# A graph layer with experts: another order in the prologue, gate columns first, and residuals of the last tiles on TensorE

## The chip, the cores and the metric
One core of a Trainium2 chip. The metric is the device time of one execution in microseconds, the lower the better; three executions of the kernel before took 656.91, 658.34 and 659.75 us (median 658.34).

## The reference
2500 nodes with 512 numbers each, 80000 edges (src, dst), sorted by dst. All in fp32.

```python
h = layernorm(x)
agg = segment_sum(h[src], dst, 2500)
x = x + relu((h + agg) @ W1 + b1) @ W2 + b2          # W1, W2: 512 x 512
t = layernorm(x)
gate = softmax(t @ Wg)                               # 8 experts
topv, topi = top_k(gate, 2); topv /= sum(topv) + 1e-6
x = x + sum_e score_e * (gelu(t @ W1[e] + b1[e]) @ W2[e] + b2[e])   # 512 -> 256 -> 512
```

## The kernel before, in words
Every engine has one program, written by hand in a fixed order; engines wait for each other on semaphores. An engine runs its instructions strictly in that order. The nodes are cut into 20 tiles of 125 rows (P = 125, T = 20). For x itself, row p * 20 + t belongs to tile t.

Stage 1, the first layer (0 to about 132 us). z = layernorm(x) @ W1 is computed before the neighbours are summed, since the sum is linear. VectorE takes the row statistics of a batch of tiles (`statistics`, BATCHES), ScalarE the root (`roots`), VectorE the reciprocal and shift (`scales`). ScalarE writes the normal rows xn (`normal_rows`, three buffers); TensorE turns them (`turn_normal`, four transposes); ScalarE copies the f16 upper part (`normal_columns`, xT_top) and VectorE takes the rest (`low_columns`, xT_rest). `first_layer(t)` on TensorE is 3 x 8 matmuls of up to 264 columns (top x W1_hi, top x W1_lo, rest x W1_hi), with `turn_normal(t + 1)` after the first 8. 8 of the columns are the gate's. `split_z` on ScalarE evicts z; GpSimd subtracts for z_lo. W1 itself is first scaled by powers of two per column: sums of absolute values (`W1_abs`, on TensorE), then `invert_scale`, `scale_weights`, `first_high` and `first_low`; `centre_gate` does the same for the gate weights.

The neighbour sum is a product with a matrix of counts. The edges are cut into 125 windows of 20 destination nodes. dst and src are loaded; for each edge a key and a source row are formed (`edge_sources`, `edge_keys`) and stored to HBM (edge_pairs). `find_chunk` finds for each window the chunk of 128 edges in which it begins, GpSimd gathers these chunks' dst rows (bound_rows), `find_starts` counts the exact start, and GpSimd gathers each window's edges as slot_rows from edge_pairs. `compare_edges`, `smallest` and `close_rows` test that the edges are of the expected form, and give a flag that goes through HBM (range_d) to all engines (a general path is taken where it is set; it isn't here). The slot rows are turned (`turn_rows`, after tile ROWS_AT = 5) and unpacked (`take_rows`). From tile FLAG_AT + 1 = 8 on, TensorE does some windows after each tile: VectorE makes the one-hots of a window (`one_hots`, hot_key and hot_lo; a ring of four), TensorE multiplies them (`window`, 6 matmuls), ScalarE evicts the counts (`take_counts`). 25 windows lie beside the tiles 8 to 19, two in each and three in the last.

Stage 2 (about 136 to 412 us). Five groups of 500 nodes: `sums_tile` multiplies z_hi and z_lo by the counts, beside it the windows of the next group; `relu`, `relu_high`, and `mlp2(g, q)`, 24 matmuls for each of the four tiles q of a group, columns 256 to 519 (gate columns among them) before 0 to 255. `logits_of` takes logits, the top 8 and their indices; `residual` adds x_res (x + b2, summed by GpSimd) to the product in PSUM, with bn_stats and bn_aggr; `std2` and `residual_end` give 1/std; `norm2` writes the normal rows xt. SP stores x and xt and loads the next residual rows.

Stage 3, the passage (412 to 458 us). For the last group `mlp2` writes to banks of its own, 0 to 7. With all 20 tiles' choices VectorE forms `chosen` and `either`; TensorE ranks them (two matmuls), VectorE computes places, at_tile, token_part and at_row; TensorE spreads them (40 matmuls), and the token lists go to GpSimd's gathers. route_tables are constants that GpSimd writes after its last residual sum. SP loads the experts 0 to 3 (512 KB twice each), then stores, expert 4, the last stores, waits until all of x has landed (x2_landed), then experts 5 to 7. ScalarE splits the weights (`split_high_up`, `split_high_down`), VectorE their lower parts.

Stage 4 (458 to 655 us): 27 blocks of 256 rows, with gathers and adds to HBM by indirect DMA. It isn't changed.

## Time and profile before

| | us |
|---|---|
| median of three executions | 658.34 |
| the profiled execution, its own time | 657.24 |
| its span, first to last instruction | 655.5 |
| TensorE busy | 555.8 (85%) |
| VectorE busy | 413.9 (63%) |
| ScalarE busy | 316.7 (48%) |
| GpSimd busy | 251.2 (38%) |
| the chain that ended last: TensorE | 50% |
| DMA, VectorE, GpSimd, ScalarE in it | 13%, 12%, 10%, 7% |

The page also has the span in 40 equal slices of 16.4 us. Each digit is the busy share in tenths, PEclk the granted TensorE clock in tenths of full speed:

```profile
PE   4776877799999999999999999925999999999900
DVE  5866574687369777976986131589566664554541
ACT  2573766533252125124322300558776766777671
PEclk9997899999899999999999999965999999999955
DMA  8160600020020310211122113779688989899995
```

The first eight slices are the first layer, slices 9 to 25 the neighbour sums with TensorE full, slices 26 to 28 the passage, then the experts. A busy share says how much an engine did, not what it waited for; the rows further down name that.

### The profile page before, as it was taken

The numbers are of one execution on the slowest core, as the hardware profiler recorded it, in microseconds if no ns is written. First come the engines' busy times: TensorE is split into PE (matmuls) and PEld (weight loads), VectorE is DVE, ScalarE is ACT, GpSimd is POOL, SyncE is SP. The second block draws the span as 40 slices with busy tenths as digits, with TensorE's granted clock in tenths as the row PEclk, the third lists the DMA queues.
The fourth block names the chain that finished last, engine by engine and source line by source line (L and its number), as shares of the span: only waits on it lengthen the run. The fifth ranks groups of instructions, "written<-read, shape, count | busy, mean of one in ns | idle before, by whom it ended". The sixth has DMA issues, their size and how long they took to land.

```text
span 655.5 us, 10719 instructions
## 1 busy us (share of the span) xinstructions
PE 555.8 (85%) x3842; PEld 435.9 (67%) x3843; DVE 413.9 (63%) x805; ACT 316.7 (48%) x579; POOL 251.2 (38%) x219
## 2 busy tenths in 40 slices
PE   4776877799999999999999999925999999999900
PEld 2666767656756766766666665725989998889800
DVE  5866574687369777976986131589566664554541
ACT  2573766533252125124322300558776766777671
POOL 4450222203016005100700331025567877778763
PEclk9997899999899999999999999965999999999955
DMA  8160600020020310211122113779688989899995
GB/s 259 54 161 1 192 1 1 1 75 1 1 64 2 95 48 12 84 48 49 49 77 65 39 58 96 262 236 304 139 172 183 186 167 193 187 205 198 165 185 76
DMA packets 40302, 71.91 MB, mean 110 GB/s; under 512 B 10313, under 2 KB 14545, under 8 KB 39714
## 3 DMA queue, kind: packets, MB, share of 16 engines
q0 software_dynamic: 12704, 29.22, 22.6%
q1 hardware_dynamic: 26257, 37.34, 19.3%
q10 hardware_dynamic: 1288, 4.66, 2.4%
q8 instruction: 32, 0.52, 0.3%
q14 instruction: 21, 0.17, 0.1%
HBM read 46.07 MB, written 26.69 MB: 111 GB/s over the span
## 4 chain that ended last, share of the span: by engine, by line
PE 50%; DMA 13%; DVE 12%; POOL 10%; ACT 7%; issue 6%; SPq 1%; ACTq 0%; POOLq 0%; DVEq 0%
PE psum L1414 26%; PE psum L1398 9%; PE psum L1451 7%; POOL out_x L601 6%; DMA out_x<-y,target_i 6%; PE psum L1330 3%; POOL xg L594 3%; DVE hot_key L1047 2%; DMA slot_rows<-edge_pairs,start_i 2%; DVE hot_lo L1047 2%; DMA xg<-xt_d,token_i 2%; DMA b_now<-in_L_ffn_b 2%; DVE xT_rest L891 1%; DVE stat L861 1%; ACT y L823 1%
## 5 line engine op out<-in xcount | busy, mean ns | idle before, releaser
L663 ACT ACTIVATE counts<-psum 128x400 bf16<-128x400 f32 x125 | 62.6, 504 | 163.2 <-PE psum L1398 162.9
L1047 DVE TENSOR_TENSOR hot_key<-iota_key,key_w 128x1200 f16<-128x1200 f16 x125 | 105.7, 845 | 47.3 <-PE psum L1398 47.3
L1414 PE MATMUL psum<-counts,z_hi 125*128 125x500 bf16 x400 | 101.8, 375 | 1.6 <-ACT h L687 1.6
L601 POOL DMA_INDIRECT out_x<-y,target_i x54 | 88.5, 1639 | 36.3 <-SPq L480 15.0
L1414 PE MATMUL psum<-counts,z_lo 125*128 125x500 bf16 x400 | 101.5, 377 | 0.0
L1398 PE MATMUL psum<-hot_key,hot_lo 128*128 128x200 f16 x750 | 84.3, 250 | 15.6 <-DVE hot_lo L1047 14.9
L1398 PEld LDWEIGHTS psum<-hot_key,hot_lo 128*128 128x128 f16 x750 | 65.2, 98 | 39.0 <-issue 18.8
L566 POOL TENSOR_TENSOR h_lo<-h,h_hi 128x500 fp32r<-128x500 f32 x16 | 23.5, 1499 | 169.5 <-ACT h_hi L694 169.5
L1047 DVE TENSOR_TENSOR hot_lo<-iota_lo,lo_w 128x768 f16<-128x768 f16 x125 | 83.5, 668 | 0.0
L1414 PEld LDWEIGHTS psum<-counts,z_lo 125*128 125x128 f16 x400 | 39.3, 98 | 45.7 <-issue 1.1
L594 POOL DMA_INDIRECT xg<-xt_d,token_i x54 | 57.4, 1063 | 31.2 <-issue 15.5
L1261 DVE TENSOR_TENSOR he_lo<-he,he_hi 128x256 fp32r<-128x256 f32 x54 | 23.0, 425 | 66.1 <-ACT he L816 66.1
L1414 PEld LDWEIGHTS psum<-counts,z_hi 125*128 125x128 f16 x400 | 37.8, 98 | 29.3 <-ACT h L687 1.8
L1547 PE MATMUL psum<-xT_hi,w_hi 128*128 128x256 f32 x192 | 54.4, 283 | 0.3 <-DVE xT_lo L1243 0.3
L553 POOL TENSOR_TENSOR z_lo<-z,z_hi 125x512 f16<-125x512 f32 x20 | 26.9, 1352 | 71.8 <-ACT z L656 71.8
L1547 PE MATMUL psum<-xT_hi,w_lo 128*128 128x256 f32 x192 | 54.4, 283 | 0.0
L1547 PE MATMUL psum<-xT_lo,w_hi 128*128 128x256 f32 x192 | 54.4, 283 | 0.0
L823 ACT ACTIVATE y<-y,slot_score 128x512 f32<-128x512 f32 x54 | 36.0, 714 | 33.2 <-DVE y L1270 33.2
L569 POOL TENSOR_TENSOR x_res<-x_res,b_row 125x512 f32<-125x512 f32 x20 | 29.3, 1484 | 48.8 <-DMA x_res<-in_x 48.8
L1558 PE MATMUL psum<-w_hi,he_hi 128*128 128x512 f32 x96 | 40.1, 417 | 3.5 <-DVE he_lo L1261 3.1
L1270 DVE TENSOR_TENSOR y<-psum,b_now 128x512 f32<-128x512 f32 x54 | 34.6, 683 | 9.9 <-DMA b_now<-in_L_ffn_b 6.4
L1451 PE MATMUL psum<-W_hi,h_hi 128*125 128x264 f32 (+1 forms) x128 | 37.9, 296 | 0.0
(252 smaller groups left out, 1149.9 us busy)
## 6 DMA issues: line engine op xcount, KB each, us to landing
w_raw<-in_L_ffn_W SPq DMA_DIRECT2D x16, 512.0 KB, 6.8
b_now<-in_L_ffn_b SPq DMA_DIRECT2D x27, 256.0 KB, 4.9
x_res<-in_x SPq DMA_DIRECT2D x20, 224.0 KB
out_x<-x SPq DMA_DIRECT2D x20, 224.0 KB
xt_d<-xt SPq DMA_DIRECT2D x20, 224.0 KB
x_in<-in_x SPq DMA_DIRECT2D x2, 1120.0 KB
W_raw<-in_L_gnn_W ACTq DMA_DIRECT2D x2, 1024.0 KB, 5.4
out_x<-in_x SPq DMA_DIRECT2D x1, 1536.0 KB, 11.7
```

Of the source, the lines that this page charges most:

```text
L569: pool.tensor_tensor(x_res[:, q], x_res[:, q], b2_row[:], ALU.add).then_inc(S["res_sum"], 1)
L594: pool.indirect_dma_start(out=xg[:, k % XB, i], out_offset=None, in_=xt_d[:, :], in_offset=bass.IndirectOffsetOnAxis(ap=token_i[:, 2 * k + ...
L601: pool.indirect_dma_start(out=out[:, :], in_=y[:, k % YB, i], in_offset=None, out_offset=bass.IndirectOffsetOnAxis(ap=target_i[:, 2 * k + ...
L663: act.activation(counts[:, it % 2, :, place:place + W], psum[:, WIN + w % 2, 0:MW].rearrange("p (w h) -> p h w", w=W), ACT.Copy).then_inc( ...
L823: act.activation(y[:, k % YB, i], y[:, k % YB, i], ACT.Copy, scale=slot_score[:, 2 * k + i:2 * k + i + 1])\
L1047: ins = dve.tensor_tensor(hot[:, w % RING].rearrange("p s (n two) -> p s n two", two=2), iota[:].rearrange("p (o n two) -> p o n two", o=1 ...
L1270: dve.tensor_tensor(y[:, k % YB, i], psum[:, 4 + i], b2_now[:, k % 2], ALU.add).then_inc(taken, 1)
L1398: ins = mm(psum[:, WIN + w % 2, a * MH:(a + 1) * MH], hot_lo[:, w % RING, k], hot_key[:, w % RING, k], start=(k == 0), stop=(k == SL - 1))
L1414: ins = mm(psum[:, AGG + c, 0:GN], half[:, t, c * 128:(c + 1) * 128], counts[0:P, g % 2, t], start=(t == 0 and n == 0), stop=(t == T - 1 a ...
L1451: ins = mm(psum[0:P, bank + b, 0:columns.stop - columns.start], h_[:, k, rows], w_[:, k, columns], start=(k == 0 and n == 0), stop=(k == K ...
L1547: ins = mm(psum[:, 2 + m, 0:B], w_[e][:, c, cols], x_[:, c], start=(c == 0 and i == 0), stop=(c == KC - 1 and i == 2))
L1558: ins = mm(psum[:, 4 + i, :], h_[:, m, i * 128:(i + 1) * 128], w_[e][:, m], start=(m == 0 and n == 0), stop=(m == HC - 1 and n == 2))
```

## The change
It has two parts.

Prologue: the batches of row statistics are (0,2), (2,4), (4,6) and on as before. ScalarE, not VectorE, forms the edges' source rows, in three passes, before roots(0). VectorE's order puts statistics and W1's scaling first, and find_chunk(0) and (1) after low_columns(1). xn is written densely, and the turn reads it with a stride. TensorE does W1's sums before the edges' spans, and 6 + 3 extra matmuls whose result nobody reads (`stay_warm`). ROWS_AT and FLAG_AT are one tile later, so that windows begin with tile 9. In the tiles with windows VectorE makes the one-hots before low_columns(t + 1). Batch 5 of x is loaded from ScalarE's queue instead of SP's.

Passage: for the last four tiles the gate columns of all come before the other columns, and all their logits are taken together (`last_logits`). For tiles 17 to 19 TensorE adds the residual with an fp32 product by the identity, ScalarE takes the row statistics (`last_rows`), and VectorE only the reciprocal (`last_scale`). The load of the last residual rows comes before the store of tile 15. The first half of token_part is computed on VectorE; ScalarE splits experts 1 to 3 after the last normal rows.

```diff
-BATCHES = ((0, 1), (1, 3), (3, 6), (6, 10), (10, 15), (15, 20))
+BATCHES = ((0, 2), (2, 4), (4, 6), (6, 10), (10, 15), (15, 20))
-ROWS_AT, FLAG_AT, ROWS_FIRST = 5, 7, 4
+ROWS_AT, FLAG_AT, ROWS_FIRST = 6, 8, 4
...
+            sp.wait_ge(S["x2_ready"], 4 * (G - 1))
+            load_residual(G - 1, 3)
             store(G - 2, 3)
-            load_residual(G - 1, 3)
             store(G - 1, 0)
...
-                act.activation(xn[:, t % 3].rearrange("p (c q) -> p c q", c=KC), x_in[:, t % (2 * HALF)].rearrange("p (q c) -> p c q", c=KC),
-                               ACT.Identity, scale=rstd1[:, t:t + 1], bias=shift1[:, t:t + 1]).then_inc(S["xn_ready"], 1)
+                act.activation(xn[:, t % 3], x_in[:, t % (2 * HALF)], ACT.Identity, scale=rstd1[:, t:t + 1], bias=shift1[:, t:t + 1])\
+                   .then_inc(S["xn_ready"], 1)
...
+            act.wait_ge(S["src_in"], 32)
+            step(act.activation(pairs_sb[:, :, 1], src_i[:], ACT.Identity, scale=1.0 / T, bias=half_down[:]))
+            step(act.activation(pairs_sb[:, :, 1], pairs_sb[:, :, 1], ACT.Identity, bias=turn_up[:]))
+            act.activation(pairs_sb[:, :, 1], pairs_sb[:, :, 1], ACT.Identity, bias=turn_down[:]).then_inc(S["sources_ready"], 1)
+            roots(0)
             first_high(0)
-            roots(0)
...
+                for b in range(1, len(BATCHES)):
+                    if t + 2 == BATCHES[b][0]:
                         roots(b)
...
+            def last_rows(q):
+                n = 4 * (G - 1) + q
+                act.wait_ge(S["mlp2_done"], n + 1)
+                act.wait_ge(x2_out[q], 64 * (G - 1))
+                step(act.activation(x2[:, q].rearrange("p (b n) -> p b n", b=2), last_out(q), ACT.Copy, accum_out=last_ln[:, q, 0:1]))
+                step(act.activation(last_ln[:, q, 1:2], last_ln[:, q, 0:1], ACT.Copy, scale=-1.0 / D))
+                step(act.activation(xt[:, q], x2[:, q], ACT.Square, bias=last_ln[:, q, 1:2], accum_out=last_ln[:, q, 2:3]))
+                act.activation(last_ln[:, q, 3:4], last_ln[:, q, 2:3], ACT.Sqrt, scale=1.0 / D, bias=eps_t[0:P, 0:1]).then_inc(S["std2_ready"], 1)
...
             std2(G - 2, 3)
             split_high_up(0)
             norm2(G - 2, 3)
             split_high_down(0)
+            std2(G - 1, 0)
+            last_rows(1)
             norm2(G - 1, 0)
+            last_rows(2)
+            last_norm(1)
+            last_rows(3)
+            last_norm(2)
+            last_norm(3)
+            for e in range(1, 4):
+                split_high(e)
...
-            centre_gate()
-            find_chunk(0)
+            largest()
+            statistics(0)
             invert_scale()
             scale_weights(0)
-            statistics(0)
             scale_weights(1)
             scales(0)
             scale_weights(2)
             scale_weights(3)
+            centre_gate()
             first_low(0)
             first_low(1)
-            find_chunk(1)
             low_columns(0)
+            edge_keys()
             statistics(1)
             scales(1)
-            edge_sources()
             low_columns(1)
-            edge_keys()
+            find_chunk(0)
+            find_chunk(1)
+            low_columns(2)
             statistics(2)
-            low_columns(2)
             scales(2)
+            low_columns(3)
             scale_back()
             find_starts()
...
             for t in range(FLAG_AT + 1, T):
+                for w in range(counted(t - 1), counted(t)):
+                    one_hots(w)
                 if t + 1 < T:
                     low_columns(t + 1)
-                for w in range(counted(t - 1), counted(t)):
-                    one_hots(w)
...
+            def stay_warm(n):
+                for k in range(n):
+                    mm(psum[:, SM + 1], part16[:].broadcast_to([128, 128]), W1_abs[:, k % KC], start=True, stop=True)
...
+            stay_warm(6)
             turn_normal(0)
+            stay_warm(3)
...
+            def add_residual(q):
+                pe.wait_ge(S["res_sum"], 4 * (G - 1) + q + 1)
+                for b in range(2):
+                    ins = mm(psum[0:P, 2 * q + b, 0:DH], ident[0:P, 0:P], x_res[:, q, b * DH:(b + 1) * DH],
+                             start=False, stop=True, skip_group_check=True)
+                ins.then_inc(S["mlp2_done"], 1)
...
+            for q in (2, 3):
+                if q == 3:
+                    pe.wait_ge(S["x2_ready"], 4 * (G - 1))
+                for k in range(KC):
+                    ins = last_gates(q, k)
+            ins.then_inc(S["gate_columns"], 1)
+            for k in range(KC):
+                last_halves(1, k)
+            pe.wait_ge(S["x2_ready"], 4 * (G - 1) + 1)
             pe.wait_ge(S["chosen_ready"], 1)
             pe.wait_ge(S["route_tables"], 1)
             choices = either[:].rearrange("p n e -> p (n e)")
             mm(psum[0:P, 0, 0:T * NE], before[:], choices, start=True, stop=True)
             mm(psum[0:P, 1, 0:T * NE], ones16[:], choices, start=True, stop=True).then_inc(S["ranked"], 1)
+            add_residual(1)
+            for q in (2, 3):
+                for k in range(KC):
+                    last_halves(q, k)
+                add_residual(q)
```

## Rows read from the trace of the kernel before
**Rows 1.** Busy time by stretch: start:end, length, each engine busy, PEclk, DMA share, GB/s.
```profile
70.00:128.00 58.00, 44.41 (x403) 40.19 (x400) 33.90 (x62) 39.86 (x73) 14.62 (x10) 1.00 0.12 37
424.00:458.00 34.00, 14.97 (x134) 14.25 (x133) 30.41 (x88) 24.57 (x31) 11.70 (x19) 0.61 0.88 278
```
**Rows 2.** The chain of waits, one first-layer tile: start us, us, what.
```profile
99.74 0.68 PE psum L1398 x6
100.42 0.89 PE psum L1330 x8
101.30 0.44 PE psum L1308 x4
101.77 0.60 ACT xT_top L646
102.39 0.68 DVE xT_rest L891
...
104.22 0.69 DVE hot_key L1047
104.91 0.48 DVE hot_lo L1047
...
105.53 0.68 PE psum L1398 x6
```
**Rows 3.** The chain of waits in the prologue.
```profile
26.21 0.68 DVE xT_rest L891
...
34.71 14.76 DMA slot_rows<-edge_pairs,start_i
```
**Rows 4.** The timeline of 10 to 25 us: start us, us, engine, line, operation.
```profile
16.07 1.30 ACT L639 ACTIVATE xn<-x_in,shift,rstd 125x512 f32<-125x512 f32 x1
...
19.20 1.99 PE L1330 MATMUL psum<-W_hi,xT_top 128*125 128x256 f16 x8 [0.68 <-ACT xT_top L646]
19.25 1.08 DVE L918 CAST chunk_i<-first 125x2 int32<-125x2 f32 x1
...
23.25 1.44 POOL L535 DMA_INDIRECT bound_rows<-in_dst,chunk_i  x1 [0.30 <-issue]
```
**Rows 5.** From the tiles bound_rows and slot_rows: time from issue to landing.
```profile
DMA to landing us min/median/max: 3.5/3.5/3.6
...
DMA to landing us min/median/max: 8.0/11.4/14.8
```
**Rows 6.** Timelines of TensorE, VectorE and GpSimd at the first layer's end.
```profile
131.87 1.20 PE L1398 MATMUL psum<-hot_key,hot_lo 128*128 128x200 f16 x12
...
135.78 1.01 PE L1414 MATMUL psum<-counts,z_hi 125*128 125x500 bf16 x4
...
128.47 1.73 DVE L1047 TENSOR_TENSOR hot_key<-iota_key,key_w 128x1200 f16<-128x1200 f16 x1
...
128.03 1.53 POOL L553 TENSOR_TENSOR z_lo<-z,z_hi 125x512 f16<-125x512 f32 x1 [4.25 <-ACT z L656]
```
**Rows 7.** The chain of waits in the passage.
```profile
426.65 2.87 DMA x_res<-in_x
...
434.35 0.33 DVE tile_count L1152
...
437.47 0.78 DVE picked L1168 x2
...
442.30 3.01 DVE at_row L1195 x5
...
458.75 3.14 PE psum L1547 x24
```
**Rows 8.** The timeline of ScalarE in the passage.
```profile
423.27 0.82 ACT L673 ACTIVATE xt<-x,ln,rstd 125x512 f32<-125x512 f32 x1
...
426.85 1.04 ACT L698 ACTIVATE w_hi<-w_raw 128x1024 fp32r<-128x1024 f32 x1
...
445.05 1.28 ACT L781 ACT_TABLE_LOAD   x1
```

More of the change, by code:

```diff
@@ L717, in _ @@
             normal_columns(0)
-            roots(1)
             normal_rows(1)
@@ L722, in _ @@
                     normal_columns(t + 1)
-                for b in range(2, len(BATCHES)):
-                    if t == max(BATCHES[b][0] - 3, 1):
+                for b in range(1, len(BATCHES)):
+                    if t + 2 == BATCHES[b][0]:
                         roots(b)
@@ L1119, in _, with last_logits, last_scale @@
                             residual_end(g - back, q)
+            def last_logits():
+                dve.wait_ge(S["gate_columns"], 2)
+                for q in range(4):
+                    n = 4 * (G - 1) + q
+                    ins = dve.tensor_tensor(logits[:, n], psum[0:P, 2 * q + 1, DH:DH + NE], gate_in[:, n], ALU.add)
+                step(ins)
+                for n in range(4 * (G - 1), T):
+                    ins = dve.max(top[:, n], logits[:, n])
+                step(ins)
+                for n in range(4 * (G - 1), T):
+                    ins = dve.max_index(topi[:, n], top[:, n], logits[:, n])
+                step(ins)
+            def last_scale(q):
+                n = 4 * (G - 1) + q
+                dve.wait_ge(S["std2_ready"], n + 1)
+                step(dve.reciprocal(rstd2[:, n:n + 1], last_ln[:, q, 3:4]))
+                dve.tensor_tensor(last_ln[:, q, 4:5], last_ln[:, q, 1:2], rstd2[:, n:n + 1], ALU.mult).then_inc(S["shift2_ready"], 1)
             for m in range(KC):
@@ L1123, in _ @@
                 dve.tensor_tensor(last_lo[:, m], h1[:, m], last_hi[:, m].bitcast(F32), ALU.subtract).then_inc(S["h1_split"], 1)
-            logits_of(G - 2, 3)
+                if m == 2:
+                    logits_of(G - 2, 3)
             residual(G - 2, 3)
-            for q in range(3):
-                logits_of(G - 1, q)
-                residual(G - 1, q)
-                residual_end(*((G - 1, q - 1) if q else (G - 2, 3)))
-            residual_end(G - 1, 2)
-            logits_of(G - 1, 3)
+            residual(G - 1, 0)
+            residual_end(G - 2, 3)
+            residual_end(G - 1, 0)
+            last_logits()
             def split_low_up(e):
@@ L1430, in mlp2 @@
             def mlp2(g, q):
-                last = g == G - 1
-                bank = (WIN, AGG, AGG + 2, SM)[q] if last else SM
-                if q == 0 and not last:
+                if q == 0:
                     pe.wait_ge(S["w_split"], 1)
@@ L1497, in _ @@
             mlp2(G - 2, 3)
-            for q in range(4):
-                mlp2(G - 1, q)
+            for k in range(KC):
+                pe.wait_ge(S["h1_split"], 4 * (G - 1) + k + 1)
+                last_gates(0, k)
+                ins = last_halves(0, k)
+                if k == 1:
+                    last_gates(1, 0)
+                if k == KC - 1:
+                    ins.then_inc(S["mlp2_done"], 1)
+                if k >= 1:
+                    last_gates(1, k)
+            for q in (2, 3):
[3 more added lines that the diff above has]
+                    ins = last_gates(q, k)
+            ins.then_inc(S["gate_columns"], 1)
+            for k in range(KC):
+                last_halves(1, k)
+            pe.wait_ge(S["x2_ready"], 4 * (G - 1) + 1)
             pe.wait_ge(S["chosen_ready"], 1)
```

148 lines of the change are left out of this document (73 added, 75 removed).

## The prediction
> **What bounds the kernel now.** First the table by stages: from 70 to 128 us TensorE is busy 44.4 of 58 us at a granted clock of 1.00 (2.4 GHz), so the stretch of tiles 8 to 19 of the first layer is full of waits, while from 424 to 458 us it is busy 15 of 34 us at a mean granted clock of 0.61, since it waits long, and VectorE 30.4 of 34 [rows 1]. The expert loop behind it isn't touched. Between 135.8 us, where the neighbour sums start [rows 6], and 412 us TensorE is fed back to back and the change moves nothing. So two stretches decide: the prologue (0 to 135.8) and the passage to the experts (412 to 458.75).
>
> Then the chain of waits. In one tile of the first layer it goes round: windows 0.68, first third of the layer 0.89, the turn of the next tile 0.44, ScalarE's xT_top 0.60, VectorE's xT_rest 0.68, only then the one-hots, 1.16 each (104.22 to 105.4), and again the windows, at 105.53: 5.79 us from 99.74 to 105.53 [rows 2]. The one-hots of tile t stand behind low_columns(t+1) in VectorE's order, which needs the turn of tile t+1. That is a loop of waits, no engine's work. Ahead of it stands the chain that makes the edge rows: chunk_i done at 20.33, start_i at 32.4, the second gather issued at 34.71 and landed 14.76 us later, at 49.47 [rows 3, 4].
>
> **Prologue, part by part.**
> Early order. Statistics of two tiles, W1's sums and the scaling go ahead of the search for chunks. low_columns(1) ended at 26.89 [rows 3]. I bring it forward by 3.6 to about 23.3: W1's sum no longer waits behind the edge spans (about 1.8 us, an estimate from the order of the steps), and the 24 matmuls of tile 0, at 0.25 each (1.99 for 8, against 0.89 for 8 later: that is the lower of the clock's two levels, 1.2 against 2.4 GHz) [rows 2, 4], take 2.7 instead of 5.5 us if stay_warm does what it says. Bound: 0 to 4 us. Against that stand ScalarE's three passes over the sources, 640 elements each; they were 0.5 us each on VectorE and need at least 0.82 x 640/512 = 1.0 us [rows 8], at most the strided xn's 1.30 x 640/512 = 1.6 [rows 4]. I take 1.2; they start when src has landed (estimate 10 us) and hold roots(0), so that I keep 1 us of the 4.6 for them, which is the 3.6.
> The two find_chunk steps, some 3.1 us, now follow low_columns(1): chunk_i is known at 26.4 instead of 20.33, 6.1 later. Before, the second bound gather was issued at 23.25 and took 3.5 [rows 4, 5]; now 29.35 and 32.9. VectorE used to arrive only at 31.4, so 4.7 of the 6.1 were slack; behind the landing stand a rest of low_columns(3) and the two counts. start_i is at about 34.4, 2 us later than 32.4; the slot gather's second half is issued at 36.7 instead of 34.71 [rows 3].
> Queues. It was slow (14.76) beside dst_next and x_in's batch 4 on SP's queue. The keys leave 8 us earlier, so dst_next is over, and batch 4 is asked for at about 33.6, ahead of the gather. The other half of the gather landed in 8.0 [rows 5]. Bounds 8 and 14.8; I take 10.8, as one of the two disturbers is left: landed at L = 47.5 (44.7 to 51.5) against 49.47.
> From L to the first window. One tile more goes ahead (FLAG_AT 8). By L all of tiles 0 to 6 are done (3.1 us of matmuls each [rows 2], no waits for dst_next now). (These counts are mine, from the order of the program.) After L: close, turn and take the rows, statistics(4), scales(4); these steps took 15 us before and take 12.6 now, as low_columns(8) and one fewer handshake lie between; xn(10) 0.8, turn 0.5, two thirds of the layer 1.8: windows of tile 9 at L + 15.7 = 63.2.
> The loop. VectorE now makes the one-hots of tile t first, while TensorE does tile t. TensorE's own work is 3 x 0.89 + 0.44 + 2 x 0.52 = 4.15 us with two windows [rows 2]; a tile with three windows waits some 0.85 for the counts to be taken, 5.5. ScalarE has 0.48 + 0.75 (xn dense, 0.82 like norm2 [rows 8], instead of 1.30 [rows 4]) + 1.24 + 0.9 = 3.4; VectorE 2 x 1.16 + 0.6 = 2.9. So TensorE sets it: 7 x 4.15 + 2 x 5.5 + 3.7 (no turn) = 43.7, and 2.7 for statistics(5) and its scales, which still stand on VectorE's path: 46.4 to the end of tile 19, at 109.6. Before it was 131.87 [rows 6]. Reading xn with a stride in the turn costs 0.01 to 0.02 per transpose, nothing. The sums start 3.9 later in both. **Gain 22.3 us**, bounds 14 (below) to 26.
>
> Here a rule is weighed. Rows: a hot_key that ran beside a z_lo of GpSimd took 1.73 where it takes 0.69 to 0.77 [rows 2, 6], about 0.95 more. The Trainium skill's GPSIMD Engine Reference (specification table, SBUF interfaces) says that GpSimd shares its SBUF interfaces with VectorE, with contention for instructions with two SBUF inputs, which the one-hots are; by that rule z_lo, which used to fall into VectorE's idle time, now meets a one-hot in each tile. The trace agrees for that row.
> With one meeting in each tile VectorE has 3.9, still under 4.15: hidden, so the sum has nothing for it. Cover gone, it is the first rival.
>
> **Passage to the experts, part by part** (times as if the prologue were unchanged).
> Gate columns first: TensorE has all logits of tiles 16 to 19 by 422.8. VectorE reaches last_logits only at 424.65, since residual_end(G-1,0) waits for a std2 queued on ScalarE behind a split of expert 0, norm2 and another split. 1.8 for logits, max and index, 1.8 for the choice: chosen_ready 428.2 against 431.9.
> But ranking also waits for route_tables, on GpSimd behind x_res of the last tile. That load is now issued at 420.3 instead of 426.26, behind four experts' weights on SP's queue (4.2 MB, an estimate from the sizes has them over at about 426). I take it as landed at 426.7; it was 429.52 [rows 7]. tile_count followed 4.83 behind it, at 434.35 [rows 7]; now 431.5, a gain of 2.85 (0 if the queue is slower, 5.4 if chosen_ready alone decided).
> Residual by TensorE: the first add stands behind the ranking, so mlp2_done(18) comes at 431.5 + its price. No row shows an fp32 matmul that wide. Bounds: two cold passes of 0.25 (0.5) and eight (2.0) [rows 4]; I take 1.5, for fp32 is the slowest type here: 433.0. Then 12 matmuls, cold: 2.9; add 1.2; 12 warmer: 1.5; add 1.0: 437.2 and 439.6.
> ScalarE's last_rows: copy 0.8 with the sum, 0.25, square 0.9, root 0.3, three handshakes: 2.5 (2.1 to 3.0), from 0.82 for 512 elements [rows 8]. std2 of tiles 17, 18, 19 come at 435.6, 439.7, 442.9.
> VectorE waits for each: last_scale(1) comes 2.9 after tile_count (picked was 3.12 after it [rows 7]) at 434.4 and waits 1.2; last_scale(2) 1.8 behind the next step at 437.8 and waits 1.9; last_scale(3), at 441.9, waits 1.1. Then token_part's first half, now on VectorE: 1.0 (0.7 to 1.3); second half 1.3; at_row from 445.8 instead of 442.30, five in 3.0 [rows 7]. So routing is 3.5 us later. Taking away the residuals (three of 1.65) from VectorE is worth nothing here: the waits are longer.
> ScalarE stands idle from 424.3 to 433, with the splits of experts 1 to 3 (six of 1.04, 0.95 apart [rows 8]) queued behind last_norm(3) at 444.4; before, four of the six were in gaps up to 437.6. It gets to Exp at about 451.4 (447.35 before), then the Gelu table 1.28 [rows 8], the splits 4 to 7, 7.6, and xT_hi at 460.9. SP's stores land later, so x2_landed and the last three experts' loads shift too, 448.8 instead of 440.8, which just holds. The first expert matmul, 458.75 [rows 7], is at 462.8. **Loss 4.0 us** (gain 1 to loss 8).
>
> One rule of the ScalarE page is weighed. The rows have a table load of 1.28 where Exp and where Gelu first come [rows 8], none between Sqrt and Copy, Identity or Relu; Square is not in the trace. If it isn't beside Sqrt, each last_rows has two loads: 6 x 1.28 = 7.7 on a chain that VectorE waits for. The Trainium skill (ScalarE: Activation LUTs, Table sets: the hidden batching unit) has the cheap functions in every set, by which there is none. No run here shows it.
>
> **Sum.** The profiled execution took 657.24 us (span 655.5), 0.17% below the median of 658.34. 657.24 - 22.3 + 4.0 = 638.9; on the median's scale 640.
>
> **Rivals.**
> 1. VectorE becomes the bound of the tile loop: two meetings with z_lo in each tile, 2.9 + 1.9 = 4.8 and 6 with three windows, 0.65 more in each of 10 tiles plus the statistics unhidden: +8, 647 to 648. For: z_lo (1.53) is as long as a one-hot pair [rows 6] and starts right when the one-hots do. Against: one z_lo can delay only the instruction it meets. Chance 0.20.
> 2. The passage costs nothing: the fp32 adds are near their lower bound, the clock rises early, and x_res lands when it can. Then 4 to 5 less: 635. For: 8 us of slack on ScalarE. Against: ScalarE's splits stay behind. Chance 0.17.
> 3. stay_warm doesn't raise the clock, or the long gather stays long (L = 51): tile 0 costs 2.8 more, L 3.5 more: 646. Chance 0.13. Square's table loads: 648. Chance 0.04.
> 4. Slower: the new order in the loop turns round on itself. If VectorE falls a whole tile behind, low_columns(t+1) stands behind the one-hots and TensorE's last third waits for it: 0.89 + 0.44 + 0.60 + 2.3 + 1.9 + 0.68 + 0.89 + 1.0 = 8.7 us per tile against 5.79 now [rows 2]. 63.2 + 10 x 8.7 = 150 against 131.87, and 4.0 lost in the passage: 680. It turns to slower from (131.87 - 63.2 - 4.0)/10 = 6.5 us per tile. For it: VectorE's 3.9 is only 0.25 below TensorE's 4.15. Against: it has to lose over 4 us in a row first, and the single burst that there is is statistics(5), 3.4. Chance 0.05.
>
> **How the numbers follow.** Forecast 0.41, around 640 (636 to 644). With the rivals 1, 2 and 3 the range is 632 to 651; above it lie the worst of rival 1 and rival 4, below it both gains at their bounds. 0.5% (3.3 us), about what a measurement of this kernel can tell from no change, is reached by all but rival 4 and a sum of rivals 1, 3 and a passage at -8: faster 0.91, same 0.03, slower 0.06.
>
> **What would show it.** Right: a tile period of 4.1 to 4.7 between 63 and 110 us with TensorE near 95% busy; sums starting at 113 to 114; the slot gather landing near 47; ScalarE idle for 8 us after its first split; first expert matmul 50 us after the sums end instead of 46.4. Wrong: hot_key's mean well over 1 us in the loop (rival 1), a table load in the passage, tile 0's matmuls at 0.25 each, or a gap of TensorE ahead of each last third (rival 4). The prediction fails most easily in the loop: ten tiles carry each error tenfold.

## The result and the profile after

| | before | after |
|---|---|---|
| median, us (20 runs each, 655.14 to 661.31 and 650.93 to 657.60) | 657.84 | 653.96 |
| ratio to before, 95% interval | | 0.9939 [0.9921, 0.9958] |
| the profiled execution, its own time | 657.24 | 656.98 |
| its span | 655.5 | 655.2 |

The change gives 4 us where 18 were forecast, and 653.96 lies above the range (632 to 651). The profiled execution of after lies 3.0 us above its median; all stage times below come from it, so some 3 us of what it lacks against the forecast belong to this one execution.

The 40 equal slices of after, 16.4 us each:

```profile
PE   5788989999999999999999999424999999999900
...
PEclk9899989998999999999999999776899999999965
DMA  8253300200012202211120335379487999899996
```

The first eight slices of TensorE read 57889899 where they read 47768777 before, so the first layer is denser; the dip of the passage is deeper, 424 against 925. Busy time by stretch in after, to be read as [rows 1]: TensorE was busy 77% of 70 to 128 us before, now 90%; in the passage it is 52% of 62 us.

```profile
70.00:120.00 50.00, 45.09 (x412) 43.19 (x411) 44.10 (x71) 34.52 (x76) 16.31 (x12) 0.97 0.03 7
398.00:460.00 62.00, 32.20 (x237) 29.85 (x236) 33.74 (x104) 35.83 (x57) 13.71 (x23) 0.75 0.69 224
```

The same in times. Offsets in the last four rows are counted from the start of the last matmul of the sums (412.23 before, 398.45 after).

| | before | after | the step on record |
|---|---|---|---|
| chunk_i | 20.33 | 27.43 | 26.4 |
| start_i | 32.4 | 37.87 | 34.4 |
| first windows beside a tile | 69.44 (tile 8) | 68.39 (tile 9) | 63.2 |
| sums start | 135.78 | 121.30 | 113.5 |
| tile_count, behind the sums | 22.1 | 21.5 | 19.3 |
| last store of normal rows issued | 25.8 | 35.1 | |
| x2_landed (load of expert 5 issued) | 28.6 | 39.2 | 36.6 |
| first expert matmul | 46.5 | 59.2 | 50.6 |

So in this pair of executions the prologue gives 14.5 us (forecast 22.3) and the passage takes 12.7 of them back (forecast 4.0). The sums (276.5 and 277.2) and the expert blocks (196.8 and 197.6) hardly differ. The chain of waits of after, through the passage (start us, us, what):

```profile
406.92 8.24 DMA x_res<-in_x
415.23 1.26 POOL x_res L578
419.94 1.80 PE psum L1503 x4
433.52 3.91 DMA xt_d<-xt
440.27 13.48 DMA w_raw<-in_L_ffn_W
454.74 1.04 ACT w_hi L710
456.30 1.30 DVE xT_lo L1276 x2
457.64 5.50 PE psum L1620 x24
```

Before, the chain went over at_tile, token_part, at_row and the table load [rows 7, 8], that is over the routing. Now it goes over the residual rows, the adds on TensorE (L1503), the last store, and then the weights of an expert. The weights weren't in the chain before. The prediction had said of their later loading that it "just holds"; it doesn't. ScalarE, which splits each expert's weights in its fixed order, shows it: in after it waits 2.02, 4.26 and 1.89 us for weights on their way (8.2 in all), in the trace of before it doesn't wait for any.

### The profile page after: what moved, and what is told of

Same layout as the page of the kernel before. It is cut to its first block, busy times and chain, and to the rows that moved or that the text cites. A ratio compares the mean times of both kernels' runs of the same rounds, so it can differ in the third digit from the quotient of the medians.

```text
span 655.2 us, 10782 instructions
## 1 busy us (share of the span) xinstructions
PE 565.3 (86%) x3864; PEld 446.1 (68%) x3865; DVE 416.7 (64%) x794; ACT 310.8 (47%) x596; POOL 251.0 (38%) x222
## 4 chain that ended last, share of the span: by engine, by line
PE 51%; DMA 14%; POOL 11%; DVE 7%; issue 7%; ACT 6%; SPq 1%; ACTq 1%; POOLq 0%; DVEq 0%
PE psum L1455 26%; PE psum L1439 9%; POOL out_x L610 7%; PE psum L1483 7%; PE psum L1369 6%; DMA out_x<-y,target_i 5%; POOL xg L603 4%; DMA w_raw<-in_L_ffn_W 2%; DMA xg<-xt_d,token_i 2%; DMA src_i<-in_src 1%; DMA x_res<-in_x 1%; DMA b_now<-in_L_ffn_b 1%; DVE stat L880 1%; PE psum L1347 1%; ACT y L846 1%
## 5 line engine op out<-in xcount | busy, mean ns | idle before, releaser
L1067 DVE TENSOR_TENSOR hot_key<-iota_key,key_w 128x1200 f16<-128x1200 f16 x125 | 107.7, 861 | 49.8 <-PE psum L1439 48.8
L1067 DVE TENSOR_TENSOR hot_lo<-iota_lo,lo_w 128x768 f16<-128x768 f16 x125 | 86.4, 691 | 0.0
L562 POOL TENSOR_TENSOR z_lo<-z,z_hi 125x512 f16<-125x512 f32 x20 | 26.7, 1344 | 52.5 <-ACT z L665 52.5
L1620 PEld LDWEIGHTS psum<-xT_hi,w_hi 128*128 128x128 f32 x192 | 37.8, 197 | 8.9 <-DVE xT_lo L1276 8.0
L1276 DVE TENSOR_TENSOR xT_lo<-psum,xT_hi 128x512 fp32r<-128x512 f32 x56 | 36.1, 686 | 10.4 <-ACT xT_hi L814 8.7
```

Source lines behind the costliest of these rows:

```text
L1067: ins = dve.tensor_tensor(hot[:, w % RING].rearrange("p s (n two) -> p s n two", two=2), iota[:].rearrange("p (o n two) -> p o n two", o=1 ...
L1276: dve.tensor_tensor(xT_lo[:, :, part], psum[:, i].rearrange("p (c n) -> p c n", c=KC), xT_hi[:, :, part].bitcast(F32), ALU.subtract).then_ ...
L1620: ins = mm(psum[:, 2 + m, 0:B], w_[e][:, c, cols], x_[:, c], start=(c == 0 and i == 0), stop=(c == KC - 1 and i == 2))
```

## Experiments

Each was timed beside the kernel before on the same chip, but not all on one chip (the medians of before were 656.3 to 657.8). So two changed kernels are compared by their ratios to before: "ratio to after" is the quotient of the two. A profile is one execution; kernels with the very same prologue (after, e1, e3, e5, e7) started their sums at 118.3 to 122.5, so a difference under some 4 us in the start of the sums says little by itself.

**e1 and e2: the two halves of the change.** The edit of e1 is the change's diff without its passage parts, e2 the rest.

> The kernel before with the changed prologue and tile loop only; the passage to the experts as before. Theory (the two halves of the change are separate, and their sizes are those of the two traces): the sums start 14.5 us earlier and the passage takes its old 46.2 us from the end of the sums to the first expert matmul, so the time is 14 to 15 us under the kernel before, ratio 0.978. Rival (the prologue's gain is real, but an earlier start makes something behind it slower, so the passage would lose even with its old order): the sums start 14.5 us earlier, but the passage takes 50 us or more, ratio 0.985 to 0.993.

Measured: 641.21, ratio 0.9741 [0.9715, 0.9767]. The sums start at 122.48, 13.3 earlier; first expert matmul 46.6 behind them, as before.

> The kernel before with the changed passage only: gate columns first, residuals by TensorE, row statistics on ScalarE, the new order of loads; the prologue as before. Theory: from the end of the sums to the first expert matmul 58 to 59 us instead of 46.2, and 10 to 12 us more in all, ratio 1.015 to 1.019. The step on record (a loss of 4.0) would give 1.006. If the loss in the changed kernel came from its prologue, the ratio is 1.00 here.

Measured: 672.16, ratio 1.0227 [1.0199, 1.0256]; first expert matmul 59.9 behind the sums. The halves are -16.6 and +14.4 at the medians; their sum, -2.2, agrees with the -3.9 of the whole within the intervals, and each is a little larger than the traces of the whole had it. The passage, meant as an improvement, alone makes the kernel 2.3% slower.

**e3: is it ScalarE's order?** In after, ScalarE stands idle 11.5 us for the first row sum while six splits are queued behind (timeline of ScalarE):

```profile
410.01 0.28 ACT L677 ACTIVATE ln<-ln,eps_t 125x1 f32<-125x1 f32 x1
421.76 0.60 ACT L779 ACTIVATE x<-psum 125x512 f32<-125x512 f32 x1 [11.46 <-PE psum L1503]
...
443.62 1.06 ACT L707 ACTIVATE w_hi<-w_raw 128x1024 fp32r<-128x1024 f32 x1 [2.02 <-DMA w_raw<-in_L_ffn_W]
...
449.89 1.06 ACT L707 ACTIVATE w_hi<-w_raw 128x1024 fp32r<-128x1024 f32 x1 [4.26 <-DMA w_raw<-in_L_ffn_W]
...
453.78 1.06 ACT L707 ACTIVATE w_hi<-w_raw 128x1024 fp32r<-128x1024 f32 x1 [1.89 <-DMA w_raw<-in_L_ffn_W]
```

The edit of e3:

```diff
             std2(G - 1, 0)
-            last_rows(1)
             norm2(G - 1, 0)
+            for e in range(1, 4):
+                split_high(e)
+            last_rows(1)
             last_rows(2)
...
             last_norm(3)
-            for e in range(1, 4):
-                split_high(e)
```

> The changed kernel with norm2 of tile 16 and the splits of experts 1 to 3 on ScalarE ahead of the row statistics of tile 17 instead of behind them, so that they fill its 11.5 us of idle time. Theory A (the late landing of the last tiles' stores, which holds the loads of experts 5 to 7, sets the end of the passage): the stores of tile 19 stay where they are, experts 5 to 7 still land 16 us behind x2_landed, the first expert matmul moves by under 1.5 us, ratio to the changed kernel 0.998 to 1.000. Theory B (the splits queued behind last_norm(3) set it): Exp starts 5 us earlier and the first expert matmul 4 to 5 us earlier, ratio to the changed kernel 0.992 to 0.994.

Measured: 654.95, ratio to before 0.9961 [0.994, 0.9982], to after 1.002. First expert matmul 58.4 behind the sums (59.2 in after). The splits fill the hole, and ScalarE waits later for the weights instead:

```profile
411.68 1.04 ACT L707 ACTIVATE w_hi<-w_raw 128x1024 fp32r<-128x1024 f32 x1
...
453.23 1.06 ACT L707 ACTIVATE w_hi<-w_raw 128x1024 fp32r<-128x1024 f32 x1 [3.10 <-DMA w_raw<-in_L_ffn_W]
```

Theory A holds. The 11.5 us of idle time, ScalarE's largest wait of the passage, were worth nothing that can be measured.

**e5: the residual rows in the queue.** e5 is e3 with one more edit. In after VectorE and TensorE wait for the route tables, which GpSimd writes behind the last residual rows, and these queue behind the weights of four experts (timelines of SP's queue, TensorE and VectorE):

```profile
406.54 0.79 SPq L413 DMA_DIRECT2D x_res<-in_x  x2
...
419.44 0.37 PE L1572 MATMUL psum<-either,before 125*125 125x160 f16 x1 [8.73 <-POOL goes_on L594]
...
419.98 0.32 DVE L1182 COPY tile_count<-psum 125x160 f32<-125x160 f32 x1 [6.73 <-PE psum L1573]
```

```diff
-            for e in range(4):
+            for e in range(2):
                 load_expert(e)
             sp.wait_ge(S["x2_ready"], 4 * (G - 1))
             load_residual(G - 1, 3)
+            for e in range(2, 4):
+                load_expert(e)
```

> The kernel of e3 (splits of experts 1 to 3 ahead of the row statistics), and SP loads the last tile's residual rows ahead of experts 2 and 3 instead of behind them. Theory (the ranking waits 7 us for route_tables, and these for the residual rows that queue behind 4 MB of weights): x_res lands about 5 to 6 us earlier, tile_count comes 16 us behind the end of the sums instead of 21.5 to 21.9, the stores, x2_landed, the loads of experts 5 to 7 and the first expert matmul all move by 4 to 6 us, the last to 53 to 54 us behind the end of the sums (58.4 in e3), ratio to the changed kernel 0.991 to 0.994. Rival (the load isn't held by the weights, it takes 8 us by itself): under 1.5 us of change.

Measured: 646.57, ratio to before 0.985 [0.9816, 0.9884], to after 0.991, to e3 0.989. tile_count 15.6 behind the sums, the load of expert 5 at 33.2, first expert matmul at 52.9. The ratio is as expected. Against e3 that is 7 us, the largest single repair, and it moves the loads of two experts behind a small one.

**e7: rows ahead of the ranking.** e7 is e5 with the order of the residual adds and row statistics changed (the smaller parts of the edit, on VectorE and ScalarE, are left out here):

```diff
-            for k in range(KC):
-                last_halves(1, k)
+            for q in (1, 2, 3):
+                for k in range(KC):
+                    last_halves(q, k)
+                if q == 1:
+                    pe.wait_ge(S["logits_taken"], 1)
+                if q < 3:
+                    add_residual(q)
...
-            add_residual(1)
-            for q in (2, 3):
-                for k in range(KC):
-                    last_halves(q, k)
-                add_residual(q)
+            add_residual(3)
```

> The kernel of e5, and TensorE makes the remaining column halves of tiles 17 to 19 and the residual adds of tiles 17 and 18 while it waits for the choices, ahead of the ranking instead of behind it (a wait on the logits being taken is added for the banks); VectorE takes the scales one step earlier each, ScalarE puts the splits between. Theory (the loss comes from the statistics chain of three tiles that starts behind the ranking and holds the stores, and so experts 5 to 7): x2_landed comes 30 to 32 us behind the end of the sums instead of 38.6, and the first expert matmul at 45 to 48 us instead of 58 to 59; time 10 to 13 us under the changed kernel, ratio to it 0.980 to 0.985, to the kernel before 0.974 to 0.979. Rival (the loss is in the number of handshakes between VectorE and ScalarE, wherever they stand): the first expert matmul stays at 52 us or more.

Measured: 644.79, ratio to before 0.9834 [0.9788, 0.988], to after 0.989, less than the 0.980 to 0.985 that were expected; against e5 the intervals overlap. The load of expert 5 comes at 30.2, as expected; the first expert matmul at 50.05, not at 45 to 48. Its chain still ends with the weights:

```profile
421.32 2.37 DMA xt_d<-xt
426.52 13.40 DMA w_raw<-in_L_ffn_W
440.91 1.04 ACT w_hi L712
```

The loads of experts 5 to 7 were issued 30.2 to 32.8 us behind the sums (28.4 to 31.1 in e1), and the last took 13.4 us from issue to landing (9.1 in e1). So it landed 46.2 behind the sums, 3.9 ahead of the first expert matmul. In e1 it landed at 40.2, 6.5 ahead of it, and the chain there goes over the routing. The row gathers start at 34.2 in e7, so that nearly all of the loading runs beside them, and at 36.6 in e1; that this makes the landing longer fits the traces, but wasn't tried. The new passage, with its order mended, is still behind the old one: 3.4 us by the first expert matmul (50.05 against 46.6), and 0.9% (6 us) by the ratios of e7 and e1, whose intervals lie apart.

**e4: GpSimd beside VectorE.** In after, GpSimd's z_lo and VectorE's steps in the prologue:

```profile
40.97 4.48 POOL L562 TENSOR_TENSOR z_lo<-z,z_hi 125x512 f16<-125x512 f32 x4
47.53 1.16 POOL L562 TENSOR_TENSOR z_lo<-z,z_hi 125x512 f16<-125x512 f32 x1 [2.08 <-ACT z L665]
...
42.49 2.99 DVE L890 SCALAR_TENSOR_TENSOR shift<-mv,rstd 125x4 f32<-125x4 f32 x1
...
47.70 1.67 DVE L944 TENSOR_TENSOR edge_a<-dst_i,dst_next 125x640 f32<-125x640 int32 x1
...
46.38 0.74 PE L1347 MATMUL psum<-ident,xn 125*128 125x125 f32 x4 [2.29 <-ACT xn L648]
```

A step of 4 elements per partition takes 2.99 us and ends (45.48) when the run of four z_lo ends (45.45); xn and so TensorE wait for it. edge_a starts 0.17 behind a z_lo and takes twice its time.

```diff
-                    pool.tensor_tensor(z_lo[:, t], z[:, t % ZF], z_hi[:, t], ALU.subtract)
+                    pool.memset(z_lo[:, t], 0.0)
```

> The changed kernel, with GpSimd writing zeros to z_lo instead of subtracting two operands (z_lo is left out of the result). Theory (VectorE and GpSimd hinder each other in the first layer: a shift took 2.99 us beside z_lo, one-hots 1.15 and 1.51): these instructions return to 0.2, 0.7 and 0.8 us and the sums start 3 to 5 us earlier, at 116 to 118 instead of 121.3. Rival (they merely waited for semaphores, and VectorE is off the path): the sums start within 1 us of 121.3.

e4 leaves z_lo out of the result. A memset is also shorter than the subtraction (four in 1.93 us, not 4.48), so that e4 takes away the length of GpSimd's work as well. The same two steps of e4, and the means of the one-hots up to 120 us, of after and of e4 (groups of instructions: count, busy us, mean ns; the idle time behind them is of no use here):

```profile
42.73 0.17 DVE L890 SCALAR_TENSOR_TENSOR shift<-mv,rstd 125x4 f32<-125x4 f32 x1
...
45.11 0.81 DVE L944 TENSOR_TENSOR edge_a<-dst_i,dst_next 125x640 f32<-125x640 int32 x1
```

```profile
L1067 DVE TENSOR_TENSOR hot_key<-iota_key,key_w 128x1200 f16<-128x1200 f16 x27 | 24.1, 892 | 1.0 <-issue 1.0
L1067 DVE TENSOR_TENSOR hot_lo<-iota_lo,lo_w 128x768 f16<-128x768 f16 x26 | 18.1, 696 | 0.0
```

```profile
L1067 DVE TENSOR_TENSOR hot_key<-iota_key,key_w 128x1200 f16<-128x1200 f16 x32 | 24.8, 775 | 2.7 <-PE psum L1439 1.6 <-issue 1.0
L1067 DVE TENSOR_TENSOR hot_lo<-iota_lo,lo_w 128x768 f16<-128x768 f16 x31 | 17.0, 550 | 0.0
```

Measured: 652.43, ratio to before 0.9902 [0.9874, 0.9931]. The sums start at 114.88, 6.4 earlier than in after (3.5 to 7.6 against all kernels with this prologue); windows of tile 9 at 64.89 instead of 68.39. Where VectorE is hindered is shown: the gathered edge rows (the prediction's L) landed at 49.3 in e4 and 48.9 in after, VectorE took them up at 49.30 against 51.58, and the first windows came 15.6 against 19.5 behind the landing. In the other profiles of this prologue with GpSimd's subtraction (e1, e3, e5, e7, e6, e9) they came 18.7 to 20.8 behind it. The other 2.9 of the 6.4 us lie in the tile loop (46.3 to the end of tile 19, 49.2 in after) and aren't shown to be z_lo's, since e5, e6, e7, e10 and e12 have the subtraction and took 46.6 to 47.0. By the ratios only 0.4% (2.4 us) are left of it all. Part of the difference is that loop, and the stretch from the first expert matmul to the end was 1.7 us longer in e4's profile; the rest isn't explained.

**e9: z_lo on VectorE in the loop.** GpSimd makes z_lo of tiles 0 to 8, VectorE those of 9 to 19 (vector_part(t) holds the waits and the same subtraction):

```diff
+                vector_part(t - 1)
                 if t == 11:
                     statistics(5)
```

> The changed kernel with z_lo of tiles 9 to 19 made by VectorE, between its other steps of the loop, instead of by GpSimd. VectorE gets 0.66 us more per tile, but nothing runs beside it on GpSimd. Theory (the meetings of the two engines, 0.95 us each, and not VectorE's amount of work cost the loop time): windows of tile 9 stay at 68.4, the sums start 2 to 3 us earlier, at 118 to 119.5. Rival (VectorE is the bound by its work): the sums start later, at 122 to 126, as 11 times 0.66 is added.

Measured: 654.66, ratio to before 0.9955 [0.9929, 0.9981]; sums start at 121.02. From the windows of tile 9 to the end of tile 19 it takes 46.9 instead of 49.2, but e5, e6 and e7 took 46.6 to 47.0 with z_lo on GpSimd. So the theory isn't borne out: in the loop the meetings cost nothing that can be seen. Nor is the rival: 11 times 0.66 more work on VectorE doesn't show, so VectorE has that much room.

**e6: stay_warm.**

```diff
-            stay_warm(6)
             turn_normal(0)
-            stay_warm(3)
```

> The changed kernel without the nine extra matmuls (stay_warm) around the first turn. Step on record: the 24 matmuls of tile 0 then cost 2.8 us more, at the lower clock, and the prologue ends up to 2.8 us later. Theory after the trace: TensorE falls to the lower clock again while it waits 3.7 us for chunk_i ahead of tile 1, and the chain to the slot rows goes over VectorE, so of the 2.8 us under 1.5 us reach the start of the sums, ratio to the changed kernel 1.000 to 1.003.

Measured: 655.19, ratio to before 0.9977 [0.9956, 0.9998], to after 1.004 (2.5 us; 1.2 by the medians as they stand), where 1.000 to 1.003 were expected; the two intervals just touch. The sums start at 121.10 (121.30 in after). A small gain by stay_warm is neither shown nor excluded; the timeline of TensorE in after has why it isn't larger:

```profile
21.35 1.05 PE L1369 MATMUL psum<-W_hi,xT_rest 128*125 128x256 f16 x8
...
27.58 1.96 PE L1369 MATMUL psum<-W_hi,xT_top 128*125 128x256 f16 x8 [3.72 <-DVE chunk_i L937]
```

The clock rises (eight matmuls in 1.05, the 2.4 GHz level; the first eight of tile 0 took 1.71, in e6 1.97) and after 3.72 us of waiting they take 1.96 again (1.2 GHz).

**e11 and e13: the order in the tile loop**, taken out of the change, and put alone into the kernel before. The diff of e13 (e11 is its reverse):

```diff
-                if t + 1 < T:
-                    low_columns(t + 1)
                 for w in range(counted(t - 1), counted(t)):
                     one_hots(w)
+                if t + 1 < T:
+                    low_columns(t + 1)
```

> The changed kernel, but in the tile loop VectorE again makes low_columns(t+1) ahead of the one-hots of tile t, as before the change; everything else as changed. Theory (the loop of waits cost some 1.2 us in each tile, and this one order of two steps removes it): the tiles take 5.4 to 5.8 us each again instead of a mean of 4.9, the sums start 5 to 8 us later, at 126 to 129 us, ratio to the changed kernel 1.008 to 1.012. Rival (the gain came from the order of the early steps alone): the sums start within 2 us of 121.

Measured: 675.5, ratio to before 1.0311 [1.0276, 1.0346], to after 1.037. The sums start at 141.00, 19.7 later than in after, not 5 to 8. Two-window tiles take 5.84 as expected; two tiles with three windows take 9.0 and 9.8, since their windows wait for one-hots one by one and TensorE falls to the lower clock (timeline of TensorE in e11):

```profile
89.83 0.68 PE L1439 MATMUL psum<-hot_key,hot_lo 128*128 128x200 f16 x6 [1.36 <-DVE hot_lo L1067]
90.99 0.68 PE L1439 MATMUL psum<-hot_key,hot_lo 128*128 128x200 f16 x6 [0.48 <-DVE hot_lo L1067]
92.16 0.95 PE L1439 MATMUL psum<-hot_key,hot_lo 128*128 128x200 f16 x6 [0.49 <-DVE hot_lo L1067]
92.90 1.94 PE L1369 MATMUL psum<-W_hi,xT_top 128*125 128x256 f16 x8
...
98.80 0.68 PE L1439 MATMUL psum<-hot_key,hot_lo 128*128 128x200 f16 x6 [1.22 <-DVE hot_lo L1067]
```

Before, only the last tile had three windows. The step of FLAG_AT from 7 to 8 makes three such tiles out of 11, and this is a cost that the new order has to pay for first; how much of the 19.7 it is, was not tried.

> The kernel before, with one edit: in the tile loop VectorE makes the one-hots of tile t ahead of low_columns(t+1). Nothing else of the change. Theory (the period of 5.79 was a loop of waits over this one order, and e11 showed what it is worth when it is missing): periods of 4.15 to 4.3 us, 3 to 6 us for the statistics of batch 5 and the meetings with z_lo, so the 12 tiles from 69.4 take 50 to 53 us instead of 66.3 up to the start of the sums, which comes at 119 to 123; ratio to the kernel before 0.975 to 0.981, nearly all of what the whole prologue gives (0.974). Rival (the order pays only together with the earlier chain to the slot rows and dense xn): sums start after 126, ratio 0.985 or more.

Measured: 640.40, ratio 0.9755 [0.9731, 0.978]. Sums start at 119.72. This one swap gives as much as the whole new prologue (e1: 0.9741); the intervals overlap nearly whole. The timeline of TensorE in e13, one tile in 4.12 us without a wait, against 5.79 in [rows 2]:

```profile
95.83 1.19 PE L1398 MATMUL psum<-hot_key,hot_lo 128*128 128x200 f16 x12
96.86 1.05 PE L1330 MATMUL psum<-W_hi,xT_top 128*125 128x256 f16 x8
...
99.06 1.05 PE L1330 MATMUL psum<-W_hi,xT_rest 128*125 128x256 f16 x8
99.95 1.19 PE L1398 MATMUL psum<-hot_key,hot_lo 128*128 128x200 f16 x12
```

**e12 and e10: start_i, and the mended load with the old passage.** e12 is e1 with

```diff
             statistics(2)
+            find_starts()
             scales(2)
             low_columns(3)
             scale_back()
-            find_starts()
```

> The kernel of e1 (new prologue, old passage) with find_starts directly behind the statistics of batch 2, ahead of their scales, low_columns(3) and scale_back. Theory (start_i came 3.3 us later than the step on record since find_starts stood behind scales(2), which waited 2.8 us for ScalarE's roots, and not since the bound rows were late): start_i 2.5 to 3.2 us earlier, the second slot gather lands at 46 to 47 us. Of that only what the chain of VectorE lets through reaches the end: the close of the rows stood behind compare_edges and the meetings with z_lo, so the sums start 0 to 2.5 us earlier, ratio to e1 0.996 to 1.000. Rival (VectorE just waits for the bound rows instead, and TensorE waits for low_columns(3) behind it): no gain, or 1 us lost.

Measured: 637.93, ratio to before 0.9713 [0.9691, 0.9734], to e1 0.997 (1.8 us); the intervals of the two overlap for the most part, so a gain over e1 isn't shown. start_i comes at 35.33, 2.5 earlier than in after, but the second gather took 11.4 us instead of 9.2 and landed at 48.6, not at the 46 to 47 that were expected. What came earlier is VectorE behind it (49.07 instead of 51.58): the run of z_lo that waits behind the gathers on GpSimd is now from 38.44 to 42.94, and shift, begun at 41.78, takes 1.18 instead of 2.99, again up to the end of that run. The sums start at 116.28, 6.2 earlier than in e1's profile; 2.1 of these lie in the tile loop, which wasn't changed.

e10 is e12 with the loads of e5 in the old passage.

> The kernel of e12, and in the old passage SP loads the last tile's residual rows ahead of experts 2 and 3, as in e5. Theory (with the old order the choices are known only 19.4 us behind the end of the sums, and the ranking waited only 0.9 us for route_tables, so that the load is worth little here, unlike in the changed passage): tile_count 0.5 to 1.5 us earlier, the first expert matmul 0 to 1.5 us earlier, ratio to e12 0.998 to 1.000. Rival (the load is worth its 6 us in any order): first expert matmul at 42 us behind the end of the sums instead of 46.6.

Measured: 638.15, ratio to before 0.9727 [0.9701, 0.9752]. tile_count 21.9 (22.1 in e12), first expert matmul 46.3 behind the sums. No gain: the same swap that was worth 7 us in the new passage is worth nothing in the old one, where the choices come later than the tables.

e12 and e10 are the fastest of all and can't be told apart: both some 18 us under before on their chip, and by the ratios 14 to 15 us under after.

## Why the prediction was wrong, step by step

*Where the time is lost against the sum.* The profiled execution took 656.98 where the sum was 638.9. Of the 18.1 us the prologue is 7.8, the passage 8.6, the sums 0.7, the expert blocks 0.9. At the medians it is 14 us (653.96 against 640).

*Early order.* chunk_i came 1.0 later than forecast; stay_warm raised the clock, but a gain by it isn't shown (e6). A step that failed is start_i at 34.4: it was 37.87 (32.4 before, 2.3 ahead of the issue in [rows 3]), since find_starts stood behind scales(2), which waited 2.81 us for a root that ScalarE makes behind normal_columns. The prediction had the slack of VectorE there, but not ScalarE's place. e12 takes 2.5 us of it back, and the landing of the rows hardly moved, so this miss decided little.

*From L to the first window.* L, the landing of the second gather, was near 48.9 (the gathers were issued at 38.18 and 39.72 and took 7.1 and 9.2), inside its bounds. But L wasn't what the close of the rows waited for: VectorE got there only at 51.58, and the windows came 19.5 behind L, not 15.7. This stretch is the step of the prologue that failed. The 3.8 are the meetings with z_lo: without the subtraction the windows came 15.6 behind L (e4), as forecast. They were weighed as a rival for the loop alone; in the chain ahead of it GpSimd works off four z_lo at once, behind the gathers for which it was waiting, and that is where the worst meeting is (e4: windows 3.5 earlier). Rival 1 had the right mechanism at the wrong place, and the argument against it, that one z_lo can delay only the instruction it meets, doesn't hold for four in a row.

*The loop.* The period is right: a tile takes 4.15 to 4.17 where nothing disturbs it, 4.12 in e13. The whole loop took 49.2 us to the end of tile 19 against 46.4 forecast, but that isn't the rule: after, e1 and e3 took 48.9 to 49.2, and seven other kernels with the same order on TensorE (e4, e5, e6, e7, e9, e10, e12) 46.3 to 47.0. The difference is in one place, the three-window tile that statistics(5) holds up. TensorE waits 1.07 there in after and falls to the lower clock, in e5 it doesn't (timelines of TensorE, after and e5, the first eight matmuls of the next tile; the granted clock from 85 to 88 us was 0.50 in after and 1.00 in e5):

```profile
85.79 1.94 PE L1369 MATMUL psum<-W_hi,xT_top 128*125 128x256 f16 x8
```

```profile
85.69 1.05 PE L1371 MATMUL psum<-W_hi,xT_top 128*125 128x256 f16 x8
```

So the term for the loop was nearly right, its 2.7 for statistics(5) included, and the 2.8 that are over in after come with that fall. Why some kernels have it and others don't is open.

*What was the prologue's gain made of?* The prediction didn't part its 22 us between the two orders. e13 shows that the loop's order alone gives 16 us, the early order on top of it nothing that can be measured. What it gains (one tile more ahead) it seems to pay with the three-window tiles and with chunk_i 7 us later; that is read from the traces and wasn't tried.

*The passage.* The choices were known at 14.5 behind the sums (forecast 16.0; 19.3 before). The step that failed first: x_res, forecast to land 14.5 behind the sums, was to bring tile_count to 19.3; the load took 8.24 us behind the weights and landed at 16.7, tile_count came at 21.5, and the gates' head start of 5 us bought 0.6. The routing behind it caught up (at_row begins at 33.1, forecast 33.6), and ScalarE's work came as forecast (Exp at 39.3, forecast 39.2).

Second, and larger, is x2_landed. It was forecast 8 us later than before and came 10.6 later, and that this "just holds" was a guess without a sum. The first expert matmul is x2_landed (39.2), 2.6 until the last load is issued, 13.5 until it lands, and 3.9 for its splits and the first block's: 59.2 behind the sums, which is what was measured. The rows of before would have given a warning: there the last load was issued 3.0 behind x2_landed and took 9.0, so it landed at 40.6, and ScalarE came to split it only at 42.7. There were 2.1 us of slack, and the forecast moved the loads by 8 and ScalarE by 4. Its own 36.6 with 3.0, 9.0 and 3.9 makes 52.5, not 50.6. So of the 8.6 us some 2 could have been worked out beforehand, 2.6 are the stores, which were later still, and 4.5, less 0.4 for the quicker issue, are the landing, 13.5 instead of 9.0. It is long (12.1 to 14.5) in all profiles with the new passage, where the row gathers start with these loads (39.6 behind the sums in after), and 9.0 or 9.1 in before, e1, e10 and e12, where they start some 5 us behind the last one; the cause wasn't tried apart.

The cause of the late stores is the one that the prediction names itself, residuals behind the ranking; it followed it to VectorE's waits (1.15, 0.74, 0.64 measured, 1.2, 1.9, 1.1 forecast) and not into SP's queue. e5 and e7 confirm the path: with x2_landed at 33.2 and 30.2 instead of 39.2 the first expert matmul came at 52.9 and 50.05.

*Small terms.* The adds on TensorE took 1.8 us for four instructions at the lower clock (taken: 1.5; 0.9 later on), last_rows 2.1 of ScalarE's time each (2.5 with the handshakes), the first half of token_part 0.80 (1.0), no table load for Square: right. None of them decided.

*Rivals.* Rival 2 (the passage costs nothing) is refuted by e2, rival 3 by the trace of after (the clock rose, and the second gather took 9.2), rival 4 (the loop turns round on itself) didn't occur; the slower half was the passage, for which the prediction had no rival with a price beyond 8 us.

## What to carry to other kernels

Before an engine is relieved, ask of each late consumer what its last input is, and write the sum down to a transfer's landing: a wait of 11.5 us filled (e3) gave nothing, loads swapped in a queue (e5) gave 7, and the same swap with another order of the work (e10) nothing. Where a wait circle is seen in a loop, undo it alone first: one swap of two steps (e13) held the whole gain of the prologue. An operation of GpSimd that "has time" costs VectorE's short steps the length of its whole backlog, so see where a queue of it is let loose.

## What the hardware showed that was not expected

VectorE's instruction isn't slowed beside a GpSimd z_lo, it is held up to the end. In every profile with the new prologue and the subtraction shift met four of them back to back and ended 0.02 to 0.04 us behind the run; two of them: 42.49 + 2.99 = 45.48 against 40.97 + 4.48 = 45.45 (after), 41.78 + 1.18 = 42.96 against 38.44 + 4.50 = 42.94 (e12). The other way round too: a z_lo of after, begun at 82.80 among the one-hots, took 2.91 where it takes 1.16. The Trainium skill (SBUF — State Buffer, SBUF: two separate sides) calls the port pair that the two engines share an exclusive lock, which the one that starts first has for its whole instruction while the other is blocked. The trace agrees, and goes beyond it: one z_lo is 1.16, VectorE was held for 2.99, so the lock wasn't handed over between two instructions of the run. The same page restricts it to VectorE's instructions with two SBUF inputs or in a two-port mode; a copy of 40 elements with one input, which took 0.18 in e4, took 1.12 in after and ended with a z_lo (51.77 + 1.12 = 52.89 against 51.70 + 1.15 = 52.85). Whether it ran in such a mode the trace doesn't say.

Issuing transfers costs the engine that issues: two loads of x rows, moved to ScalarE's queue, took 2.40 us there, and the eviction behind them waited 1.64:

```profile
65.16 2.40 ACTq L352 DMA_DIRECT2D x_in<-in_x  x2
67.61 0.60 ACT L661 ACTIVATE z_hi<-psum 125x512 f16<-125x512 f32 x1 [1.64 <-issue]
```
